# A gated expert layer and a gated transformer block in fp32: Q/K copies, product order and work split in the attention stage

## What is computed

```python
x = x + tanh(g_xattn) * experts(layernorm(x), ids)          # token picks 1 of 4 experts
x = x + tanh(g_ffn)   * block(layernorm(x))

def block(hidden):                                           # per sequence, 512 tokens
    a = rmsnorm(hidden, ln1)
    q, k, v = (a @ W.T in 16 heads of 32, for Wq, Wk, Wv)
    p = softmax(causal(q @ k.T / sqrt(32)))                  # 512 x 512, lower triangle, per head
    attn = (p @ v in all heads) @ Wo.T
    mod = 0.1 * tanh(attn @ A)                               # A is 512 x 16
    h = rmsnorm(hidden, ln2)
    gate = silu(h @ W_in.T + mod * (h @ A) @ B)              # 2048 wide
    return hidden + (gate * (h @ W_up.T)) @ W_down.T
```

## Time and profile before

| what | value |
|---|---|
| median of 3 runs | 1078.74 us (1078.07 to 1079.66) |
| the profiled execution | 1080.39 us, its span 1078.7 us |
| PE matmul busy | 1035.0 us, 96% |
| DVE busy | 735.5 us, 68% |
| ACT busy | 613.1 us, 57% |
| POOL busy | 177.7 us, 16% |
| mean granted TensorE clock | 0.997 of full speed |

### The profile page before, as it was taken

The page is one execution under the profiler, slowest core; times in us unless marked ns, Lnnn a source line. Parts: engine busy times, 40 slices in busy tenths (PEclk is TensorE's granted clock), DMA queues, the critical chain, the costliest instruction groups (busy, mean ns, idle before and its releaser), DMA issues.

```text
span 1078.7 us, 17949 instructions
## 1 busy us (share of the span) xinstructions
PE 1035.0 (96%) x5336; PEld 860.9 (80%) x5337; DVE 735.5 (68%) x1662; ACT 613.1 (57%) x1463; POOL 177.7 (16%) x156
## 2 busy tenths in 40 slices
PE   6999999999999999989999999999999999899998
PEld 6787878777888888878888888778888877788887
DVE  7766747996665559985664589966655689854443
ACT  4464547886444458875444378864354588754342
POOL 4536122320000003320000024200000133200000
PEclk9899999999999999999999999999999999999999
DMA  6534132443322425243322354432234342333221
GB/s 244 188 141 165 39 118 70 97 100 120 105 88 90 151 69 140 64 119 128 108 89 88 108 142 97 112 117 88 88 102 141 85 121 68 79 91 105 88 88 49
DMA packets 47063, 115.59 MB, mean 107 GB/s; under 512 B 6800, under 2 KB 6800, under 8 KB 46096
## 3 DMA queue, kind: packets, MB, share of 16 engines
q1 hardware_dynamic: 43968, 105.06, 33.1%
q0 software_dynamic: 3040, 9.96, 2.7%
HBM read 76.46 MB, written 13.37 MB: 83 GB/s over the span
## 4 chain that ended last, share of the span: by engine, by line
PE 80%; DVE 9%; issue 3%; DMA 3%; ACT 2%; SPq 1%; POOL 1%; DVEq 0%; ACTq 0%; POOLq 0%
PE bank L510 64%; PE bank L709 4%; PE bank L722 3%; DVE wr L1326 3%; DVE nb L1338 3%; PE bank L681 3%; DMA stack<-wr 2%; PE bank L758 1%; SPq L307 1%; DVE big L1347 1%; PE bank L685 1%; ACT big L962 1%; PE bank L769 1%; PE bank L566 1%; DMA big<-in_x,gidx 1%
## 5 line engine op out<-in xcount | busy, mean ns | idle before, releaser
L510 PE MATMUL bank<-hT,wr 128*128 128x512 f32 x1488 | 358.4, 390 | 0.0
L510 PEld LDWEIGHTS bank<-hT,wr 128*128 128x128 f32 x1488 | 278.9, 188 | 59.9 <-issue 1.3
L510 PE MATMUL bank<-wr,actr 128*128 128x512 f32 (+1 forms) x1224 | 303.3, 397 | 2.2 <-DVE actr L1308 1.5
L510 PEld LDWEIGHTS bank<-wr,actr 128*128 128x128 f32 x1224 | 229.1, 190 | 51.1 <-issue 3.3
L1376 DVE SCALAR_TENSOR_TENSOR wr<-stream,lns,wr 128x256 fp32r<-128x256 f32 x256 | 122.3, 538 | 51.0 <-ACT wr L1001 51.0
L1326 DVE TENSOR_TENSOR wr<-bank,wr 128x512 fp32r<-128x512 f32 (+1 forms) x224 | 124.6, 600 | 19.7 <-ACT wr L878 19.7
L962 ACT ACTIVATE big<-bank,nb 128x512 f32<-128x512 f32 (+3 forms) x256 | 131.7, 531 | 9.7 <-DVE nb L1338 8.2
L878 ACT ACTIVATE actr<-act_sb 128x512 fp32r<-128x512 f32 x64 | 40.4, 632 | 145.7 <-DVE act_sb L1390 145.7
L878 ACT ACTIVATE wr<-bank 128x512 fp32r<-128x512 f32 (+1 forms) x224 | 102.6, 532 | 27.8 <-PE bank L510 18.7
L1013 ACT ACTIVATE sil<-bank 128x512 f32<-128x512 f32 x64 | 38.1, 596 | 137.6 <-PE bank L758 137.6
L485 POOL TENSOR_SCALAR big<-big,rr 128x256 f32<-128x256 f32 x64 | 78.0, 1219 | 205.9 <-DVE rr L1343 205.9
(11 more groups left out here) (182 smaller groups left out, 1078.6 us busy)
## 6 DMA issues: line engine op xcount, KB each, us to landing
stream<-in_wmlp SPq DMA_DIRECT2D x64, 512.0 KB, 4.0
stack<-wr SPq DMA_DIRECT2D x192, 128.0 KB, 2.3
stream<-in_wmlp SPq DMA_DIRECT2D x64, 256.0 KB, 2.7
big<-in_x SPq DMA_DIRECT2D x4, 1024.0 KB, 5.5
big<-y_rows SPq DMA_DIRECT2D x4, 1024.0 KB, 5.6
residual<-big SPq DMA_DIRECT2D x4, 1024.0 KB, 5.1
big<-residual SPq DMA_DIRECT2D x4, 1024.0 KB, 5.6
out<-big SPq DMA_DIRECT2D x3, 1024.0 KB, 4.5
```

What stands on the lines that cost most here:

```text
L510: mm = pe.matmul(dst, lhs(pl, k), rhs(pr, k), start=start and i == 0, stop=stop and i == n - 1, skip_group_check=skip)
```

## The change

Two `qk` buffers are used in turn, so that the wait on stack loads goes two quads back. Q and K of a later quad are made in halves of six matmuls, one half in each of heads 0 to 8; the first half for K of quad 1 is done ahead of head 0. The rounding copy and low part of K of the next quad come at the end of the step j = 0, those of Q of the quad after it at the end of the step j = 2, on ACT and DVE. The Q/K weights of quads 2 and 3 are rounded on GpSimd and no longer on ACT, and each quad's are handled as two instructions (Q, K). Probability rows 0 are scaled on GpSimd and no longer on ACT; rows 2 move from DVE to GpSimd and rows 1 from GpSimd to DVE. The up product of chunk 0 is spread over six heads (9 to 14) in parts of two matmuls. The first K product of a batch, the second half of the values and the zeroing matmul change bank or place, and the loops over quads are written out. `vst` loses 64 unused columns per tile.

```diff
-FIRST_QK = (6, 7)
-VALUES, LOW_RANK = (4, 7), 5
+FIRST_QK = (6, 3)
+VALUES, LOW_RANK = (4, 6), 5
-NORM_DVE, NORM_ACT, NORM_POOL = (3, 2), (0,), (1,)
+NORM_DVE, NORM_POOL = (3, 1), (0, 2)
+UP_PARTS = 6
+UP_FROM = H - 1 - UP_PARTS
-        qk = carve(6144, 2048).rearrange("p (m t) -> p m t", m=4)
+        qk = carve(6144, 4096).rearrange("p (n m t) -> p n m t", n=2, m=4)
...
-                with sp.Fori(1, NQ) as q:
+                for q in range(1, NQ):
...
+            def weights_high(b, q, which):
+                pool.wait_ge(qk_done, (b * NQ + q - 1) * 2 + which + 1)
+                g.tensor_copy(wqs[:, HI, which, :, :], wqk_v[:, which, :, q * P:q * P + P]).then_inc(wq_hi, 1)
+
+            def weights_low(b, q, which):
+                pool.wait_ge(wq_hi, (b * NQ + q) * 2 + which + 1)
+                g.tensor_tensor(wqs[:, LO, which, :, :], wqk_v[:, which, :, q * P:q * P + P],
+                                wqs[:, HI, which, :, :].bitcast(F32), ALU.subtract).then_inc(wq_lo, 1)
...
                     for j in range(QH):
                         if q < NQ - 1 or j < QH - 1:
                             normalise((b * NQ + q) * QH + j + 1)
-                        if j == 1 and q < NQ - 2:
-                            weights_low(b, q + 2)
+                        if j < 2 and q < NQ - 2:
+                            weights_high(b, q + 2, j)
+                            weights_low(b, q + 2, j)
...
     PE, project:
-                    pe.wait_ge(wq_hi, n + 1)
-                    pe.wait_ge(wq_lo, n + 1)
-                    if which and to == QKB:
-                        pe.wait_ge(qk_lo, n * 2 + 1)
+                    pe.wait_ge(wq_lo, n * 2 + which + 1)
+                    if q:
+                        pe.wait_ge(qk_lo, n * 2 + which)
     PE, turn_probs:
+                    elif first and kt == 2:
+                        pe.wait_ge(vpb_ok, values_out)
     PE, head_step:
-                if j == 2 and ahead == 2:
-                    project(b, q + 2, 0, half=0)
-                if j == 0 and ahead:
-                    project(b, q + 1, 1)
-                if j == 3 and ahead == 2:
-                    project(b, q + 2, 0, half=1)
+                if j == 0 and q < NQ - 1:
+                    project(b, q + 1, 1, half=1)
+                elif j and q < NQ - 2:
+                    project(b, q + 2, (0, 0, 1)[j - 1], half=(0, 1, 0)[j - 1])
...
-                    up_part(0, ((0,), (1,), (2, 3))[j])
+                    up_part(0, head - UP_FROM)
     PE, batch:
                 values((0, 1))
+                pe.matmul(bank[ATT][:, :], zeror[:, :], hT[:, HI, 0, :], start=True, stop=False, ...)
...
-                turn_probs(b * H, 0, first=True)
+                turn_probs(b * H, 0, first=True, values_out=b + 1)
                 scores(b * H + 2, 0, b * (H // 2) * 48 + 96)
-                pe.wait_ge(vpb_ok, b + 1)
-                pe.matmul(bank[ATT][:, :], zeror[:, :], hT[:, HI, 0, :], start=True, stop=False, ...)
+                project(b, 1, 1, half=0)
     ACT, split_qk:
-                if which == 0 and not first:
+                if which == 0 and q >= 2:
                     for k in range(2):
-                        act.wait_ge(stk[k], n * 96)
-                copy(qk[:, (Q_HI, K_HI)[which], :], bank[at][:, :]).then_inc(qk_hi, 1)
+                        act.wait_ge(stk[k], (n - 1) * 96)
+                copy(qk[:, q % 2, (Q_HI, K_HI)[which], :], bank[at][:, :]).then_inc(qk_hi, 1)
     ACT, head_step:
                     exponentials(n + 1, (j + 1) % 2)
-                    normalise(n + 1, (j + 1) % 2)
-                if j < 2 and ahead:
-                    split_qk(b, q + 1, j)
                 for i, (bk, w, at) in enumerate(((4, 512, 0), (5, 512, 512), (6, 256, 1024))):
                     act.wait_ge(p_turned, n * 3 + i + 1)
                     copy(pts[:, j % 2, HI, at:at + w], bank[bk][:, 0:w]).then_inc(pt_hi, 1)
                 if j == 0:
...
+                if j == 0 and q < NQ - 1:
+                    split_qk(b, q + 1, 1)
+                elif j == 2 and q < NQ - 2:
+                    split_qk(b, q + 2, 0)
     ACT, batch, behind the first exponentials:
-                normalise(b * H, 0)
+                split_qk(b, 1, 0)
     DVE, head_step: the low parts of Q and K move in the same way
     from behind the scaling of rows to the end of the step, and in
     batch, quad 1's Q goes behind the scaling of head 0:
                 normalise(b * H, 0)
+                qk_low(b, 1, 0)
                 maxima(b * H + 1)
```

More of the change, by code:

```diff
@@ L299, in load_stack @@
                     sp.wait_ge(qk_lo, g * 2 + 2)
-                elif type(q) is int and j == 1:
+                elif q == 0 and j == 1:
                     pass
@@ L468, in _ @@
                 if i == ITEMS - 4:
[L469 to L479, removed]
+                    for which in range(2):
+                        weights_low(0, 0, which)
             def normalise(n):
@@ L487, in _ @@
             for b in range(NB):
-                weights_low(b, 1)
+                for which in range(2):
+                    weights_low(b, 1, which)
                 normalise(b * H)
@@ L494, in _ @@
                             normalise((b * NQ + q) * QH + j + 1)
-                        if j == 1 and q < NQ - 2:
-                            weights_low(b, q + 2)
+                        if j < 2 and q < NQ - 2:
+                            weights_high(b, q + 2, j)
+                            weights_low(b, q + 2, j)
                 if b < NB - 1:
-                    weights_low(b + 1, 0)
+                    for which in range(2):
+                        weights_low(b + 1, 0, which)
         @block.tensor
@@ L724, in attend, with head_step @@
                 mm.then_inc(pv_done, 1)
[L726 removed]
+            def head_step(b, q, j):
                 n = (b * NQ + q) * QH + j
[L731 to L737 removed]
+                head = q * QH + j
+                if j == 0 and q < NQ - 1:
+                    project(b, q + 1, 1, half=1)
+                elif j and q < NQ - 2:
+                    project(b, q + 2, (0, 0, 1)[j - 1], half=(0, 1, 0)[j - 1])
+                if head < H - 1:
                     turn_probs(n + 1, (j + 1) % 2)
[L739 to L740 removed]
+                if UP_FROM <= head < H - 1:
+                    if head == UP_FROM:
                         pe.wait_ge(qk_lo, (b + 1) * (NQ * 2))
@@ L744, in head_step @@
                         pe.wait_ge(cg_lo, b * NCH + 1)
-                    up_part(0, ((0,), (1,), (2, 3))[j])
-                if ahead or j < QH - 3:
+                    up_part(0, head - UP_FROM)
+                if head < H - 3:
                     m = b * (H // 2) + q * 2 + (j + 3) // 2
@@ L763, in up_product, with up_part @@
                               lambda p, k: hT[:, p, k, :], DT).then_inc(u_done, 1)
[L765 to L772, removed]
+            def up_part(par, part):
+                n = DT * len(PARTS) // UP_PARTS
+                for i in range(part * n, part * n + n):
+                    k, (pl, pr) = i // len(PARTS), PARTS[i % len(PARTS)]
+                    mm = pe.matmul(bank[UP[par]][:, :], wch[:, par, pl, (DT + k) * P:(DT + k) * P + P],
+                                   hT[:, pr, k, :], start=i == 0, stop=i == DT * len(PARTS) - 1,
+                                   skip_group_check=True)
+                if part == UP_PARTS - 1:
                     mm.then_inc(u_done, 1)
@@ L814, in batch @@
                 values((0, 1))
+                pe.matmul(bank[ATT][:, :], zeror[:, :], hT[:, HI, 0, :], start=True, stop=False,
+                          skip_group_check=True).then_inc(pv_done, 1)
                 pe.wait_ge(qk_lo, b * (NQ * 2) + 2)
@@ L823, in batch @@
                 pe.wait_ge(ha_ok, b + 1)
-                turn_probs(b * H, 0, first=True)
+                turn_probs(b * H, 0, first=True, values_out=b + 1)
                 scores(b * H + 2, 0, b * (H // 2) * 48 + 96)
-                pe.wait_ge(vpb_ok, b + 1)
-                pe.matmul(bank[ATT][:, :], zeror[:, :], hT[:, HI, 0, :], start=True, stop=False,
-                          skip_group_check=True).then_inc(pv_done, 1)
-                with pe.Fori(0, NQ - 2) as q:
+                project(b, 1, 1, half=0)
+                for q in range(NQ):
                     for j in range(QH):
[L832 to L835, removed]
+                        head_step(b, q, j)
                 pe.wait_ge(exp_ok, (b + 1) * H * 4)
@@ L943, in split_wqk, with split_qk @@
             def split_wqk(b, q):
-                copy(wqs[:, HI, :, :, :], wqk_v[:, :, :, bass.ds(q * P, P)]).then_inc(wq_hi, 1)
-            def split_qk(b, q, which, first=False, at=QKB):
+                for which in range(2):
+                    copy(wqs[:, HI, which, :, :], wqk_v[:, which, :, q * P:q * P + P]).then_inc(wq_hi, 1)
+            def split_qk(b, q, which, at=QKB):
                 n = b * NQ + q
```

(29 more changed lines are left out.)

25 lines of the change are left out of this document (11 added, 14 removed).

## The result

The changed kernel takes 1122.6 us as a median (1118.8 to 1123.9) against 1079.2 for the kernel before: ratio 1.039, 95% interval 1.036 to 1.042, so 43 us slower where 21 were forecast. One more execution of it took 1324.0 us at a granted clock of 0.75 and is left out of the comparison. The profiled one took 1123.9 us and has a span of 1121.8 us and a mean granted clock of 0.983 of full speed; before it was 0.997.

What follows compares the result with a forecast made beforehand. PE was taken to set the pace only narrowly, with DVE about as slow. Terms of 0.8 + 4.2 + 0.5 = 5.5 us a batch, 22.0 over four, less 1.15, gave +20.9: median 1100 us, main range 1094 to 1107.

Steps and rivals of the forecast that it cites:

- The deciding step: Heads 0, 2, 4, 6, 8: ACT's copy awaits its product ahead of needed exponentials; PE waits 1.6 us, step 6.55.
- Rival 1: Heads 0 to 8: the copies cost no wait and heads run at 4.66 us; 1066 us less 1.15, chance 0.08.
- The batch's start: Start of each batch: six K matmuls ahead of head 0, partly offset by removed waits; +0.8 us, between 0 and 1.5.
- the wait of 1.15 us in batch 3: Head 1 of batch 3: PE's wait for its stack load would vanish, -1.15 us once.
- the forecast's own signs of being wrong: Profile signs that would refute it: pairs near 9.3 us, ACT busy up to the copy, or PE waiting for GpSimd.
- A pair is 11.2 and four pairs 44.8, against 40.54: +4.2: Heads 0 to 7 of each batch: pairs of a 6.55 us and a 4.66 us step, costing 4.2 us more.
- The unrolled loops put new code in front of each queue; only SP's showed such a cost: Written-out loops on all queues: only SP would pay, and it has 2 us to spare, so no cost.
- The late heads: Heads 8 to 15: period 4.55 us in heads 9 to 12, end at 33.6 against 33.07, +0.5 us a batch.
- Rival 2: Late heads: DVE and ACT relief shows, period 4.15 us, 2.5 us a batch less; 1090 us, chance 0.13.
- rival 3: Odd and late heads: GpSimd scaling of 4 us makes transposes 0.6 us late; +24, 1124 us, chance 0.05.
- The estimate from columns: GpSimd row scaling, 128 + 384 columns for 256: bounds 1.2 and 3.05 us, taken as 1.8 a head.
- port sharing might eat DVE's gain: Row scaling: a shared SBUF port might cancel DVE's 0.1 us a head, making heads 9 to 12 0.4 a batch higher.

Runs made afterwards that it cites:

- filled_wait: Changed kernel plus six zero matmuls on PE in front of the scores of heads 0, 2, 4, 6 and 8; 1109.8 us, ratio 1.030.
- late_copies: Changed kernel with ACT's Q and K copies behind the next step's exponentials and DVE's low parts behind its next scaling; 1078.8 us, ratio 1.0001.
- late_k_only: Changed kernel with only K's copies and low parts (heads 0, 4, 8) moved one step later, Q's left; 1097.1 us, ratio 1.018.
- before_k_end: Kernel before with only K's copy and low part moved to the end of step j = 0; 1104.4 us, ratio 1.024.
- before_unrolled: Kernel before with only the loops over quads written out on SP, PE, ACT and DVE; 1081.9 us, ratio 1.003.
- late_up_first: late_copies with the two up matmuls of heads 9 to 14 put ahead of the transposes; 1073.3 us, ratio 0.995.
- before_wide_rows: Kernel before with only the changed kernel's row scaling (0 and 2 on GpSimd, 3 and 1 on DVE, none on ACT); 1075.8 us, ratio 0.9965.
- late_rows_3_2: late_copies with probability rows 3 and 2 scaled on DVE and rows 0 and 1 on GpSimd; 1077.3 us, ratio 0.9978.

## Why the prediction was right and wrong

**The deciding step was right.** A step whose product and copy meet was put at 6.55 us with a wait of 1.6, a pair at 11.2. At the full clock the trace has T = 448.23 to 459.40 for heads 4 and 5, 11.17, and waits of 1.63 (K) and 1.76 (Q). `filled_wait` has 44.9 for heads 0 to 7 where 44.8 was forecast. That the place of the copies causes it is shown by three runs: late_copies takes all of it away, late_k_only its share, before_k_end makes it in the kernel before. Each of them moves ACT's copy and DVE's low part together, so their halves aren't tested apart; the trace points at ACT, whose exponentials end each wait. Rival 1 (the copies ride free) is refuted. The batch's start came out as forecast too, but for the longer program below: from the transposes of head 0 to head 0's own six matmuls it takes 0.9 us more, where 0.8 was forecast (408.90 to 411.61 before; 418.94 to 421.12, and 1.4 for six matmuls, after). Of the wait of 1.15 us in batch 3 nothing is left in the new trace. None of the forecast's own signs of being wrong showed: pairs near 9.3, ACT busy up to the copy, PE waiting for GpSimd.

**The step that failed: the clock was put at nothing.** The size of the loss was about half of what came, and the largest missing term stands in the step "A pair is 11.2 and four pairs 44.8, against 40.54: +4.2". It priced every matmul at the granted clock that the earlier trace rows show. With 1.6 to 1.8 us of idle PE every 11 to 13 us the clock fell to 0.50 for some 3 us behind 11 of the 20 waits. In batch 1 the four pairs take 12.7, 12.9, 11.2 and 12.9. PE's chain from head 0 to head 8 is 49.6 and not 44.8, and filled_wait gives back 12.8 us of the whole. The Trainium skill (TensorE: Matmul & The Clock Gate, Part 1: The HAM clock gate) describes a gate on PE's clock that goes by how busy PE has been. The rows agree, with 1.00 before a wait of 1.63 us and 0.50 about 1 us behind it, and I had not weighed it. Why it fell behind 11 of the waits and not behind the other 9, which look the same, these runs don't show. The clock isn't the whole error: with it at 1.000 filled_wait still takes 1109.8 us, 10 above the forecast.

**A second term put at nothing: the longer program.** "The unrolled loops put new code in front of each queue; only SP's showed such a cost" was wrong for PE: before_unrolled costs 3.4 us, of which PE's four waits are 3.1. That the waits are for instructions to be loaded is argued from the q8 packets and the absence of any releaser, not shown apart.

**The late heads were mis-sized a little.** Forecast 33.6 from head 8 to the end; measured 506.6 - 472.3 = 34.3. The period was put at 4.55 and is 4.6, the transposes of head 10 came at 7.5 as forecast, and head 15's waited 0.37 us for a low part, which I had at none. The rest is the last `attend`: it starts 3.0 us behind those transposes and lasts 1.36, where I put 2.75 and 1.17. The reason given for the period, the up matmuls inside the loop of PE and DVE, is confirmed by late_up_first: the loop without them is 4.14, and my lower bound from DVE's work was 4.15. Rival 2 fails for this reason: the relief on ACT and DVE is real (before_wide_rows, -3.4 us) but these matmuls stood on it.

**GpSimd.** Its scaling is 2.17 us a head where I took 1.8 from bounds of 1.2 and 3.05, and nobody waited for it. So rival 3 is refuted too; that its 1124 lies near the measured 1122.6 is chance. The estimate from columns was poor: 128 columns take 946 ns beside DVE's instructions. DVE's share fell from 1.04 to 0.86, 0.18 and not 0.1. So the forecast that port sharing might eat DVE's gain didn't come true. But DVE's time doesn't follow its columns alone: its 256 take 461 ns where its 512 take 486, and its second instruction of 384 columns took 635 ns in the kernel before, with GpSimd's 256 columns beside it, and 527 in late_rows_3_2, where GpSimd's first instruction has 128 and ACT scales no rows. The cause was not tried apart.

**A trap in the new trace.** ACT's copies of Q in batches 0 to 2 are shown as released by "DMA stack<-wr" (17.9 us in six waits). The threshold that the copy waits for covers only loads of earlier quads, and the two copies of Q in batch 3 settle it: the same two semaphore waits stand in front of them, PE's projection is named as the releaser, and they start 0.03 us behind their product (917.49 to 917.52 for the first), as K's do, and not 0.17. So the landing doesn't hold them. What the batches 0 to 2 have and batch 3 has not is the loop over batches around the code; Q waits 0.13 us longer than K only there. Why is open.

The ledger: 20.9 forecast, 12.8 for the clock, 3.4 for the loops, 4 x 0.7 = 2.8 for the late heads: 39.9 of 43.4. The other 3.5 stay unplaced. The spread of the runs (1118.8 to 1123.9) is larger than that, and by the profiled executions the clock alone is worth 16.4.

## What to carry to other kernels

When a copy moves in an in-order queue, ask when its product is made and what stands behind it. Here a copy of 0.5 us, put where its product was not yet made, held the exponentials that PE needed in the same step; one step later PE never waited behind it. Once an edit opens repeated idle gaps in a matmul engine that was full, price the clock too: it cost nearly a third of the loss here. And put extra work of an engine where that engine waits anyway. Two matmuls between producer and consumer lengthened a loop by 0.46 us a head; in front of the loop's wait the same two cost nothing.

## What the runs showed of the hardware that was not expected

- PE's clock went to the 1.2 GHz level for some 3 us behind idle gaps of 1.63 to 1.77 us, but not behind each: 11 of 20 in the changed kernel (gaps 11 to 13 us apart), 5 of 12 in before_k_end and 2 of 8 in late_k_only (22 us apart). The kernel before, with gaps up to 1.17 us, kept 1.00 in these quads. Matmuls by zeros in the gap kept it at 2.4 GHz.
- A longer program with the same work cost 3.4 us, in PE waits of 0.2 to 1.2 us at the start of batches 1 and 2 and not in the first or last batch.
- On GpSimd beside DVE's scaling, 128 columns took 946 ns, 384 columns 1240; on DVE 256 took 461 and 512 took 486.
